# The last norm's stages at other places in a written-out order: window attention, feed-forward and binary convolution on one core

## What is computed

```
xa   = layernorm(x + self_attention(x))            # 8x8 windows, 8 heads
low  = layernorm(p + self_attention(p)), p = avgpool4(xa)
q    = layernorm(xa + cross_attention(xa, low))    # the low map is read in overlapping 8x8 windows
y    = layernorm(q + relu(q @ w1 + b1) @ w2 + b2)  # the last norm
out  = y + batchnorm(conv3x3(sign(y), sign(w)))    # batch statistics over all 8 images
```

## Time and profile before

| | |
|---|---|
| median of 3 runs | 2559.68 us |
| profiled execution | 2557.35 us |
| its span, first to last instruction | 2555.5 us |
| mean granted TensorE clock | 0.937 |
| instructions | 93135 |

### The profile page before, as it was taken

One profiled execution on the slowest core, in us unless ns is written; L12 is line 12 of the kernel. 1 busy time (PEld: TensorE's weight loads), 2 busy tenths in 40 slices (PEclk: granted clock), 3 DMA queues, 4 the chain that ended last, 5 costly groups with the idle time before them and its releaser, 6 DMA issues.

```text
span 2555.5 us, 93135 instructions
## 1 busy us (share of the span) xinstructions
PE 2160.4 (85%) x39704; PEld 1729.7 (68%) x39704; DVE 1596.3 (62%) x5098; ACT 1368.0 (54%) x2531; POOL 943.8 (37%) x1080
## 2 busy tenths in 40 slices
PE   6987889997999979998899979999799989898700
PEld 4776767775777757776677757777677767676400
DVE  4886766676666757776576656676567655555332
ACT  3664555664556646665455645565456544555332
POOL 3443443443344334434344433443344433333100
PEclk9999999999999989998899989999899999999955
DMA  6775655554555545554455545555455544432177
GB/s 183 210 196 162 190 147 160 168 164 125 155 165 166 154 122 165 164 158 137 132 166 151 166 120 151 160 168 143 129 162 162 161 120 118 122 113 85 44 238 261
DMA packets 335102, 393.57 MB, mean 154 GB/s; under 512 B 40033, under 2 KB 239458, under 8 KB 334690
## 3 DMA queue, kind: packets, MB, share of 16 engines
q1 hardware_dynamic: 333842, 386.62, 52.5%
q10 hardware_dynamic: 848, 0.99, 0.1%
HBM read 208.29 MB, written 160.27 MB: 144 GB/s over the span
## 4 chain that ended last, share of the span: by engine, by line
PE 58%; DVE 28%; DMA 4%; ACT 4%; issue 4%; POOL 1%; SPq 0%; POOLq 0%; DVEq 0%; ACTq 0%
PE ps_hid L672 9%; PE ps_y L683 9%; PE ps_proj L535 6%; PE ps_o L620 6%; DVE onorm L909 5%; PE ps_s L601 4%; PE ps_hid L702 3%; PE ps_s L607 3%; PE ps_t L633 3%; DVE negmax L897 3%; DVE xn L951 3%; PE ps_max L591 3%; PE ps_y L652 2%; PE ps_y L639 2%; DVE xn L932 2%
## 5 line engine op out<-in xcount | busy, mean ns | idle before, releaser
L1055 POOL TENSOR_TENSOR prob_lo<-prob,prob_hi 128x512 f16<-128x512 f32 x528 | 611.1, 1157 | 913.9 <-ACT prob_hi L770 913.9
L769 ACT ACTIVATE prob<-ps_s 128x512 f32<-128x512 f32 x528 | 313.6, 594 | 399.8 <-PE ps_s L607 394.1
L897 DVE TENSOR_REDUCE negmax<-ps_max 128x8 bf16<-128x512 f32 x528 | 360.4, 683 | 119.8 <-PE ps_max L591 115.5
L904 DVE RECIPROCAL rden<-ps_o 128x8 f32<-128x8 f32 x528 | 107.1, 203 | 518.7 <-PE ps_o L620 517.8
L909 DVE TENSOR_TENSOR onorm<-ps_o,rden 64x128 f32<-64x128 f32 x1056 | 304.9, 289 | 25.5
L770 ACT ACTIVATE prob_hi<-ps_s 128x512 f16<-128x512 f32 x528 | 313.5, 594 | 0.0
L620 PE MATMUL ps_o<-vb,prob_hi 128*128 128x68 f16 x4224 | 293.8, 197 | 3.1 <-DVE onorm L909 2.9
L672 PE MATMUL ps_hid<-xf,w_sb 128*128 128x512 f32 x512 | 286.0, 641 | 3.0 <-ACT yconv L827 2.1
L683 PEld LDWEIGHTS ps_y<-w_sb,hid 128*128 128x128 f32 x2048 | 266.5, 196 | 31.7 <-issue 26.8
L683 PE MATMUL ps_y<-w_sb,hid 128*128 128x128 f32 x2048 | 277.6, 280 | 0.6 <-ACT hid L808 0.6
L620 PEld LDWEIGHTS ps_o<-vb,prob_hi 128*128 128x128 f16 x4224 | 260.7, 100 | 9.7 <-issue 5.4
(11 more groups left out here) (106 smaller groups left out, 3554.0 us busy)
## 6 DMA issues: line engine op xcount, KB each, us to landing
k_rows<-k_flat SPq DMA_DIRECT2D x256, 256.0 KB, 3.2
qs<-q_rows SPq DMA_DIRECT2D x512, 128.0 KB, 3.2
ks<-k_rows SPq DMA_DIRECT2D x128, 512.0 KB, 4.9
q_rows<-q_flat SPq DMA_DIRECT2D x128, 256.0 KB, 2.4
vb<-v_flat SPq DMA_DIRECT2D x128, 136.0 KB, 4.2
vb<-values_out SPq DMA_DIRECT2D x128, 136.0 KB, 2.9
xin<-in_x SPq DMA_DIRECT2D x64, 256.0 KB, 3.1
self_out<-xa SPq DMA_DIRECT2D x64, 256.0 KB, 3.6
```

Of the source, the lines that this page charges most:

```text
L769: activation(prob[:, pair_no(u, k) % 2, :], ps_s[:, :], ACT.Exp)
L897: v.tensor_reduce(negmax[:, pair_no(u, k) % 2, :], ps_max[:, :].rearrange("p (a t) -> p a t", t=TOK), AX.X, ALU.max, negate=True).then_inc ...
L1055: g.tensor_tensor(prob_lo[:, i, :], prob[:, i, :], prob_hi[:, i, :], ALU.subtract).then_inc(s_prob, 1)
```

## The change

Seven numbers in the tables change: `apply2` 13.4 to 13.25, `out` 13.8 to 14.2, `out_take` 13.9 to 14.3, `out_store` 14.4 to 14.7, `conv` 14.6 to 14.85, `conv_take` 14.9 to 15.12, `conv_stats` 15.2 to 15.4, and `conv` in `LAST_CONV` 15.6 to 15.65. No instruction is added or removed.

```diff
--- before.py
+++ after.py
@@ -52,15 +52,15 @@
              v_fetch=-4.3,
              turn=4.06, turned=4.14, resid=5.1, project=5.3, stats=5.7, rstd=5.75, apply=6.6, spread=7.26,
              spread_out=7.36, h0=8.2, relu0=8.4, h1=9.2, relu1=9.4, resid2=9.45, f0=9.47, h2=10.2, relu2=10.4,
-             f1=10.3, h3=11.2, relu3=11.4, f2=11.3, f3=12.2, stats2=12.6, rstd2=12.65, apply2=13.4, out=13.8,
-             out_take=13.9, out_store=14.4, conv=14.6, conv_take=14.9, conv_stats=15.2)
+             f1=10.3, h3=11.2, relu3=11.4, f2=11.3, f3=12.2, stats2=12.6, rstd2=12.65, apply2=13.25, out=14.2,
+             out_take=14.3, out_store=14.7, conv=14.85, conv_take=15.12, conv_stats=15.4)
 LOW = dict(make_low=-9.6, q=-8.8, q_hi=-8.65, q_lo=-8.5, q_put=-8.3, q_move=-7.0, k=-7.6, k_hi=-7.4, k_lo=-7.25, k_put=-7.2,
            k_move=-6.0,
            v=-6.6, v_hi=-6.4, v_lo=-6.25, v_move=-5.8, turn=2.38, turned=2.46, resid=3.0, project=3.2, stats=3.4,
            rstd=3.45, apply=3.8, spread=4.68, spread_out=4.76, pad=5.2, expand=5.7, kk0=6.85, kk0_hi=7.05,
            kk0_lo=7.15, kk1=7.85, kk1_hi=8.05, kk1_lo=8.15, k_wrap=8.5, vv0=8.85, vv0_hi=9.05, vv0_lo=9.15, vv1=9.85,
            vv1_hi=10.05, vv1_lo=10.15, v_keep=10.5)
-LAST_CONV = dict(conv=15.6, conv_take=15.9, conv_stats=16.2)
+LAST_CONV = dict(conv=15.65, conv_take=15.9, conv_stats=16.2)
 
 
 def units_in_order():
```

## The result

The changed kernel takes 2610.89 us (median of 5 executions, 2606.32 to 2618.65), where the kernel before took 2558.87 in 5 executions on the same chip (2551.38 to 2572.14). The ratio is 1.0195, 95% interval 1.0165 to 1.0226: 52 us or 2% slower. The forecast was 2600 us, with a range of 2576 to 2624.

A forecast was written before the change was run, and what follows sets the result against it. In each period DVE's chain was taken to set the pace for some 13 us, PE for the other 19. Terms: 21.2 + 3.0 + 13.5 - 2.5 + 1.8 + 4 = 41.0 us on 2557.35; forecast 2600 us, range 2576 to 2624.

The forecast's parts named there:

- `out` behind `scores` and `rough`: Strips 1 to 5, 29 units: PE's wait goes from L691 to `v` (L560), which waits for `k_lo`; nothing gained.
- `conv_take` in strips 1 to 5: ACT's copy behind an `exp` makes DVE's `conv_stats` and PE's `turn` 0.73 us later in 29 units: 21.2 us lost.
- Strip 6: Six units: the copy behind an `exp` delays `conv_stats` by 0.50 us each, 3.0 us lost.
- The last stretch: Nine units from c47 to c59: `h3` waits for the late copy to empty its bank, 13.5 us lost.
- Strip 7: Five units: the filled wait at `out` counts, as `q` does not wait for DVE; 2.5 us gained.
- Strip 0: Five units: `out` now stands behind `turn`, both using `ps_t`; `q` starts 0.36 us later, 1.8 us lost.
- c1, c49, c50: `out` crosses `turn`, and `conv_take` holds up a hidden stage in two of them: 4 us lost, bounds 0 and 7.
- The clock: PE's falls to 1.2 GHz, 1.6 us each, taken as unchanged: 0 us, bounds -11 and +36 us.
- The third rival: The clock falls in every period of strips 1 to 5, +36 us: 2636 us; chance 0.11.
- The main term: ACT's late copy delaying `conv_stats` and `turn` by 0.73 us in 29 units of strips 1 to 5: 21.2 us.
- The gaps pay: Filling PE's wait at `out` saves 0.9 us in each of 46 units, 41 us: about 2518 us; chance 0.07.
- Absorbed on DVE: A later DVE stage absorbs the copy's delay; 24.2 us of strips 1 to 6 go: about 2576 us; chance 0.14.

The follow-up runs named there:

- experiment 1: The changed kernel with `conv_take` put back ahead of the `exp` (14.9 for 15.12), all else as changed: 2577.13 us, ratio 1.0086 against the kernel before.
- Experiment 2: The kernel before with only `conv_take` moved behind an `exp` (14.9 to 15.12): 2602.81 us, ratio 1.0176.
- experiment 3: The changed kernel with `conv_stats` moved behind `onorm` (16.1 for 15.4), the copy still late: 2597.59 us, ratio 1.0151 against the kernel before.
- Experiment 4: The changed kernel with `conv_take` ahead of the `exp` and `out` ahead of `turn` (14.055 for 14.2): 2574.34 us, ratio 1.0072 against the kernel before.
- experiment 5: The changed kernel with `out` between `scores` and `rough` (14.03) and `conv_take` ahead of the `exp`: 2572.78 us, ratio 1.0054 against the kernel before.
- Experiment 8: The kernel before with `resid2` and `f0` moved behind the following `weigh`, `scores` and `rough` (10.07 and 10.09): 2535.76 us, ratio 0.9891.
- experiment 6: The kernel of experiment 5 with the `rough` behind `out` issued three times instead of once: 2555.3 us, ratio 0.9972 against the kernel before.

## Why the prediction was right, point by point

**`out` behind `scores` and `rough`: nothing gained.** Right, though the 81.7 us that I read as PE's largest wait were 65.6 for its matmuls. The wait moved from L691 to L560, 1.13 us at `v`. Of itself it is free: experiment 1 has it in full, and its periods without a half are those of before.

**`conv_take` in strips 1 to 5: 21.2 us.** Right. 29 x (33.13 - 32.38) = 21.8. Experiment 2 shows that it needs nothing else of the change, and experiment 3 that it goes through `conv_stats`. The working holds instruction by instruction. Counted from the start of `conv`, the copy starts at 3.76 us, where the forecast had put it (1009.70 - 1005.94 in before's times); `conv_stats` at 4.39 instead of 3.66, 0.73 later; `turn` at 5.87 instead of 5.13.

**Strip 6: 3.0.** 6.2 us in the trace, 2 halves more among them; 6.2 - 3.3 = 2.9. Right.

**The last stretch: 13.5.** `h3` waits 1.42 us, where I had 1.47, and c53 grew by 1.64. 11.5 + 2 halves fewer (3.3) = 14.8, so the term was 1.3 too small. In c54 `conv` waits 0.36 us for `hid` there, where it waited 0.12 in before; that is not the copy's, since experiment 1 has it too (0.35).

**Strip 7: -2.5.** -7.0 in the trace; 3 halves fewer are 4.9 of it, which leaves -2.1, about the 0.41 us a unit of the earlier trace rows.

**Strip 0: 1.8, mis-sized.** 9.7 us in the trace. After, in unit c16, PE:

```profile
936.44 1.12 PE L633 MATMUL ps_t<-consts_sb,onorm 128*128 128x128 f32 x4 [3.20 <-DVE onorm L909]
939.19 1.12 PE L691 MATMUL ps_t<-consts_sb,xn 128*128 128x128 f32 x4 [1.64 <-ACT oT L781]
940.10 1.91 PE L535 MATMUL ps_proj<-xin,wq_sb 128*128 128x256 f32 x4
...
944.43 2.04 PE L569 MATMUL ps_proj<-kvx,wk_sb 128*128 128x512 f32 x2 [1.74 <-DVE q_flat L867]
```

I had counted `turn` at 0.66 and `out` at 0.6, their times at 2.4 GHz, where both run at half of it and take 1.12. The transposes of `out` then wait 1.64 us for the copies of `turn`. So `q` comes 1.22 us later than before, not 0.36 (measured from `stats2` in both, 10.40 against 9.18). And the half clock now reaches the first projection of the low map as well: 2.04 us, where the same instruction took 1.10. Experiment 4 gives all of it back by letting `out` go ahead of `turn`.

**c1, c49, c50: 4 us.** c49 and c50 cost 6.8, close to my upper bound of 7, with two halves more among them; c1 is 1.4 shorter with a half fewer, so the three together cost 5.4. Part is the mechanism of strip 0 (c49 takes 26.1 us before, 28.6 in experiment 1 and 27.0 in experiment 4), part the copy (c49 and c50 cost 3.2 in experiment 2, with one half more). How the rest divides is open.

**The clock, at nothing.** This term was too small, and it is the one that I had no theory for. In the trace the counts nearly even out: in strips 1 to 6 there were 8 halves before and 14 after, 9.8 us; strip 7 and the last stretch lost five, 8.2 us. Six came in strip 0. The 3 halves more ahead of c0 (6.0 us) are not the change's, as nothing of PE or ACT moved there. Over all executions the granted clock went from 0.9355 to 0.932. An estimate of its price: the time at 1.2 GHz is 2 x (1 - clock) of the span, 330 us before and 355 after. In the rows of experiment 5 a stretch of 3.40 us at 0.55 makes its period 1.63 us longer, about half of its length, so some 12 us of the 52. By the same estimate it is 18 us in experiment 1 and 17 in experiment 4, about what these two kernels lose by their medians (17 and 14). The third rival had the direction: pauses that grow bring falls. It had the size wrong, since not each of the longer pauses brings one: 11 of 29 periods have a half in after and 18 in experiment 1, 4 and 11 more than before, where the rival wanted 22 more. The late copy as such does not keep the number down: experiment 3 has it too, with periods of 32.40 us, and 18 halves. Why after has fewer than experiment 1 (its granted clock is higher by 0.0035) stays open; no run here varied the period and the 1.0 us pause at `turn` one without the other.

**The sum.** The forecast said 41 us and the medians differ by 52. The shortfall lies in strip 0 (9.7 us for 1.8), in the last stretch (1.3) and in the clock, which was put at nothing. These overlap, as strip 0's extra halves are in both. The main term was right for its reason. That the total came within 11 us is in part luck: with `out` at the same place, the estimate for the clock is 18 us in experiments 1 and 3, where after has 12.

**The rivals.** "The gaps pay" is refuted by `v`'s 1.13 us. "Absorbed on DVE" is refuted by the 1.01 us at `turn` and the period of 33.13. The Trainium skill (Perfetto Trace Analysis, Optimization Strategy) would look for the gaps of the busiest engine and what ends them; here PE's largest gap shrank by 62 us (65.6 to 3.4, matmuls alone) and the kernel lost 52. Experiment 8 shows where filling a gap pays: at a wait of PE behind which PE, and not another engine's chain, sets the pace.

## What to carry to other kernels

Where stages stand in a written-out order, ask of each moved stage whether its old place was early for somebody: the result of `conv_take` was there 0.89 us before DVE took it, and moving it 1.6 us, behind one `exp`, cost 42.6 us in all. A gap of the busiest engine is worth filling only if the next thing that this engine waits for does not end by another engine's clock: follow the chain to the next wait before counting the gain. Where short pauses cannot be removed, look at the granted clock around them, and try harmless matmuls in the pause: they made two kernels here faster by 17 us each, and the kernel before by only 3, since the same filling in a place without a pause cost some 7.

## What was unexpected of the hardware

PE's clock fell to 1.2 GHz after stretches in which PE was mostly busy: 2.59 of 3.40 us in the rows of experiment 5, and 2.35 in the earlier trace rows. It did not fall in each such place. These are windows of after, up to `v` and behind it, in a period of 33.13 us:

```profile
1027.40:1030.80 3.40, 2.27 (x62) 1.57 (x57) 3.32 (x10) 2.21 (x4) 1.50 (x2) 1.00 0.17 60
1030.80:1034.20 3.40, 3.40 (x31) 2.11 (x31) 3.29 (x15) 1.12 (x2) 2.12 (x3) 1.00 0.78 219
```

2.27 us busy, with a pause of 1.13 us in it, and the clock stayed at 1.00. So the same pause brings a fall in some periods and not in others, 11 of 29 here and 18 of 29 in experiment 1, and a kernel with such pauses has a wide spread: 34 us in experiment 5, 9 in experiment 6. In strips 1 to 5 of before, after and experiments 1 to 5 every half begins 5.0 to 6.4 us after `stats2`, near the start of `v` (5.65), and in experiment 1 they come in neighbouring periods: c10 to c13, c17 to c20, c27 to c29, c33 to c35, c42 to c45. What decides between two like periods is left open; the filled kernels show only that with the pause filled there is no fall.

The Trainium skill (TensorE: Matmul & The Clock Gate, The HAM clock gate) has the half clock come after an idle window. By that sentence experiments 5 and 6 would differ by nothing, where 17.5 us were measured. A later section of the same page (A second HAM failure mode: psum-queue depth-cycling) has a kernel whose clock swings because PE pauses often and briefly between groups of matmuls. These traces agree in kind, and put a price beside it: 1.63 us for a period of 32.4.
